# Encoder of a fusion kernel: the 82 steps of a half turn in another order

## What is computed

```python
def layer(h, p):
    q = heads(h @ wq + bq_); k = heads(h @ wk + bk_); v = heads(h @ wv + bv_)
    scores = jnp.einsum('bhqd,bhkd->bhqk', q, k) / jnp.sqrt(jnp.float32(dk))
    attn = jax.nn.softmax(scores, axis=-1)
    o = jnp.einsum('bhqk,bhkd->bhqd', attn, v)
    o = o.transpose(0, 2, 1, 3).reshape(B, S, D)
    h = _ln(h + o @ wo + bo_, g1_, bn1_)
    ff = jax.nn.relu(h @ w1 + b1_) @ w2 + b2_
    h = _ln(h + ff, g2_, bn2_)
    return (h, None)
```

## Time and profile before

| | us |
|---|---|
| median of 3 runs (4498.93 to 4503.75) | 4498.96 |
| the profiled execution | 4506.42 |
| its span, first to last instruction | 4504.5 |
| encoder, 12 turns from 424.45 to 2048.85 | 1624.40 |

### The profile page before, as it was taken

One profiled execution on the slowest core, in us unless ns is written; L12 is line 12 of the kernel. 1 busy time (PEld: TensorE's weight loads), 2 busy tenths in 40 slices (PEclk: granted clock), 3 DMA queues, 4 the chain that ended last, 5 costly groups with the idle time before them and its releaser, 6 DMA issues. The chain is left out here.

```text
span 4504.5 us, 64423 instructions
## 1 busy us (share of the span) xinstructions
PE 3885.5 (86%) x21850; PEld 2498.8 (55%) x21850; DVE 2225.2 (49%) x3415; ACT 2121.8 (47%) x3230; POOL 1103.8 (25%) x1003
## 2 busy tenths in 40 slices
PE   1799999999999999999865999999999994229998
PEld 1355555555555555555544777666676673217776
DVE  2566666666565666565615544444444441203332
ACT  0255455455454455455423766756755761003332
POOL 5123233233232233233220000000100001154443
PEclk6799999999999999999977999999999997559999
DMA  6323333323323333333105111111111113335554
GB/s 135 113 79 104 106 88 103 107 82 98 102 83 111 91 91 104 101 90 105 56 13 153 30 33 26 30 34 26 30 34 26 30 30 135 113 120 124 127 127 97
DMA packets 267379, 370.19 MB, mean 82 GB/s; under 512 B 49456, under 2 KB 168288, under 8 KB 263712
## 3 DMA queue, kind: packets, MB, share of 16 engines
q1 hardware_dynamic: 234640, 287.09, 22.7%
q0 software_dynamic: 22960, 57.40, 5.9%
q10 hardware_dynamic: 9600, 23.26, 1.6%
HBM read 236.56 MB, written 117.10 MB: 79 GB/s over the span
## 5 line engine op out<-in xcount | busy, mean ns | idle before, releaser
L691 DVE TENSOR_REDUCE mx<-ring 128x2 f32<-128x1024 f32 x768 | 919.5, 1222 | 485.1 <-PE ring L478 482.1
L605 ACT ACTIVATE probs<-ring 128x1024 f32<-128x1024 f32 x768 | 767.6, 1024 | 414.4 <-PE ring L491 413.2
L1430 DVE TENSOR_REDUCE a_nmx<-a_ring 128x1 f32<-128x561 f32 (+1 forms) x480 | 341.7, 737 | 308.9 <-PE a_ring L1271 159.4
L1320 ACT ACTIVATE a_ring<-a_ring,a_nmx 128x561 f32<-128x561 f32 (+1 forms) x480 | 333.8, 695 | 197.5 <-DVE a_nmx L1430 195.0
L478 PE MATMUL ring<-k_stack,q_stack 48*128 48x512 f32 x1536 | 359.7, 480 | 55.2 <-DVE mx L691 23.2
L491 PE MATMUL ring<-q_stack,k_stack 64*128 64x512 f32 x1536 | 358.1, 484 | 54.8 <-DVE mx L691 39.5
L505 PE MATMUL acc<-probs,vals 128*32 128x512 f32 x3072 | 396.3, 636 | 1.3 <-ACT probs L605 1.3
L1201 POOL TENSOR_SCALAR_AFFINE_SELECT a_probs<-a_probs 128x256 f32<-128x256 f32 (+1 forms) x240 | 91.9, 383 | 1221.2 <-ACT a_probs L1352 1221.2
L1352 ACT ACTIVATE a_probs<-a_ring 128x561 f32<-128x561 f32 (+1 forms) x480 | 287.3, 637 | 169.5 <-PE a_ring L1268 166.5
L1268 PE MATMUL a_ring<-a_k_hh,a_q_hl 128*128 128x256 f32 (+1 forms) x960 | 311.2, 339 | 22.7 <-DVE a_q_hl L1410 11.0
L491 PEld LDWEIGHTS ring<-q_stack,k_stack 64*128 64x128 f32 x1536 | 140.3, 189 | 282.2 <-DVE mx L691 97.7
(11 more groups left out here) (215 smaller groups left out, 6788.6 us busy)
## 6 DMA issues: line engine op xcount, KB each, us to landing
q_stack<-qk_scratch SPq DMA_DIRECT2D x576, 64.0 KB, 2.4
k_stack<-qk_scratch SPq DMA_DIRECT2D x576, 64.0 KB, 2.4
qk_scratch<-qk_hi SPq DMA_DIRECT2D x32, 768.0 KB, 3.6
qk_scratch<-qk_lo SPq DMA_DIRECT2D x32, 768.0 KB, 5.2
a_q_hm<-a_q_hl SPq DMA_DIRECT2D x48, 280.5 KB
a_k_hh<-a_k_hh SPq DMA_DIRECT2D x48, 280.5 KB
h_in<-tokens SPq DMA_DIRECT2D x34, 384.0 KB, 4.2
res<-tokens SPq DMA_DIRECT2D x32, 384.0 KB, 3.4
```

The lines of the kernel that those rows point to most:

```text
L605: nc.scalar.activation(probs[n % 2][:, pair:pair + 2, x // 2, :], buf[:, :, :], ACT.Exp, scale=DK ** -0.5).then_inc(act, 1)
L691: nc.vector.tensor_reduce(mx[s][:, i, :].rearrange("p (r t) -> p r t", r=2)[:, :, t], buf[:, :, :], AX, ALU.max).then_inc(dve, 1)
L1320: nc.scalar.activation(buf, buf, ACT.Exp, bias=nmx[0:r, i, h:h + 1], accum_out=sums[0:r, i, h:h + 1]).then_inc(act, 1)
L1430: nc.vector.tensor_reduce(nmx[0:r, i, h:h + 1], flat(buf)[0:r, 0:N], AX, ALU.max, negate=True).then_inc(dve, 1)
```

## The change

One string. Each letter stands as often as before, and the steps of each stream keep their order among themselves; no instruction is added or taken away inside the loop.

```diff
-ORDER = "jeehemehememhmepemhemheepheejeppmemememmfepmmfefmjmpjemmfmffefmepemfemfmmpmfmfjjfp"
+ORDER = "ehehejhmemehemhejempememehmpememeemfeppeemfemfmjempemfmfmpfemfmjefmmfmfmmfemppjfpj"
```

## The result

The changed kernel takes 4586.42 us (median of 4 runs, 4581.46 to 4597.36), the kernel before 4500.58 on the same chip (4 runs, 4498.93 to 4503.75). The ratio is 1.0191, 95% interval 1.0173 to 1.0209: 86 us slower, where 58 slower was predicted.

What follows compares the result with a forecast made beforehand. TensorE was taken to set the encoder's pace, with short ring-buffer waits and clock loss. Half turn +12, SyncE's queue +16 and clock +30 made +58 us on the 4498.96 median: 4557 us, range 4495 to 4600.

Steps and rivals of the forecast that it cites:

- rival 1: Longer half turn, weight-load wait and more clock loss all occur: 4557 us, range 4530 to 4590; chance 0.45.
- Part 1: Encoder half turn at full clock: 66.55 us instead of 66.13, +0.4 each, +12 us over 29; bounds 0 and +26.
- Part 2: SyncE's queue: later qk 2 delays bv, first projection of even half turns waits 1.15 us, 14 times: +16 us, bounds 0, +30.
- Part 3: TensorE's clock falls in nearly every half turn after a longer thin stretch ahead of ft: +1.05 us each, +30; bounds 0, +51.
- The walk: Stepping through the new order with step prices and the buffer-ring rule: first projection 11.15, yn 18.45, ft 25.5 us.
- The chain from `yn` to `ft`: From normalization yn, through three GpSimd sweeps, to the start of transposes ft: 7.02 us.
- the sum behind `ft`: Priced steps from ft to the half turn's end: 40.4 us plus 0.65 for a buffer wait, 41.05, against 38.52 before.
- q + 26.3: SyncE's queue: issue of the last stack, counted in us from the start q of the last projection, qk 2.
- The second: Clock falls no more often than before, costing 1.55 us a half turn; order and weight-load costs alone, 4527 us; chance 0.22.
- The third: Faster: VectorE reaches yn by 16.9, ft starts at 24.0, half turn 65.0 us, clock as before: 4483 us; chance 0.13.
- The fourth: No difference: waits only change places and SyncE's loads land in time; within 9 us of 4499; chance 0.12.
- The fifth: Dearer: longer clock fall in each half turn, weights 2.1 us late; 12 + 30 + 51 = +93, 4592 us; chance 0.08.

Runs made afterwards that it cites:

- run 12: Changed kernel with bqk loaded first on its own semaphore (no bv wait) and eight extra matmuls a half turn ahead of ft: 4503.88 us, ratio 0.9998.
- run 10: Kernel before with four extra matmuls a half turn, three ahead of place 35 and one ahead of 37: 4471.28 us, ratio 0.9934.
- run 11: Changed kernel without the bv wait, ln 1 at place 20 instead of 25, six extra matmuls a half turn: 4458.87 us, ratio 0.9899.
- run 1: Changed kernel with bqk loaded first on its own semaphore, TensorE waiting for wv and bv only at step v: 4543.93 us, ratio 1.009.
- run 7: Changed kernel without the bv wait, with twelve extra matmuls a half turn at places 30 to 35: 4518.09 us, ratio 1.0041.
- run 8: Changed kernel without the bv wait, ln 1 at place 20 instead of 25, eleven extra matmuls a half turn: 4490.39 us, ratio 0.9979.
- run 5: Control: kernel before with bqk loaded first on its own semaphore and TensorE waiting for the weights at step v: 4496.4 us, ratio 0.9999.
- run 3: Changed kernel with ln 1 moved from place 25 to 20, nothing else: 4546.9 us, ratio 1.0093.
- run 9: Changed kernel with the last projection, qk 2, moved from place 63 to 54, nothing else: 4602.07 us, ratio 1.0215.

## Why the prediction was right, and where its sizes were off

The direction, the three mechanisms and the range held, though the time lies near its upper end: 4586 of at most 4600, and rival 1, with all three parts, ended at 4590. The sum was 28 us short. Parts 1 and 2 both came out above their own upper bounds, and that the clock came out 8 us below its term, which made up for some of it, was luck. In the changed kernel's 70.69 us a half turn: 67.24 is the order with the clock up (run 12), 2.3 / 2 = 1.15 the wait for `bv`, and the rest, 2.30, the clock. Against the kernel before (66.13, none, 1.55) this is +1.11, +1.15 and +0.75, in 29 half turns 32, 33 and 22 us, together 87. The medians give nearly the same in another way: the order's price is 29 us (run 12 against run 10), the wait 32, and of the 86 this leaves 25 for the clock.

**Part 1, the undisturbed half turn: right in sign, mis-sized.** Predicted +0.4 us and 12 in all, inside bounds of 0 and 26; shown are 1.0 to 1.1 us and 29 to 32 in all, above the upper bound. The walk ran ahead by 0.4 us already at the first projection (11.15 walked, 11.56 in the profile), kept that distance to `yn` (18.45, 18.84) and `ft` (25.5, 25.85), and then lost 0.3 more behind `ft`: 41.05 walked, 67.23 - 25.91 = 41.32 measured in run 12. The chain from `yn` to `ft` was exact, 7.02 and 7.01. So the terms that failed are the head's, "the first projection (place 16) can start at 11.15", and the sum behind `ft`; which prices in them are short is not shown. The step that makes the order dear, `yn` behind three maxima, was the right one: run 11 with `yn` early takes 65.97 a half turn, run 12 without it 67.24. That is 37 us in 29 half turns; the two ratios differ by 0.0109, 49 us, and the rest isn't accounted for.

**Part 2, SyncE's queue: the mechanism right, the wait half as long as it is.** Predicted 1.15 us in 14 turns, 16 us, with an upper bound of 30; shown 2.3 and 32. The term is in the rows. A passage like most others, with `qk` 2 starting at q = 840.57 and the wait 2.25 us:

```profile
866.08 1.36 SPq L848 DMA_DIRECT2D k_stack<-qk_scratch  x3
868.25 0.41 SPq L853 DMA_DIRECT2D tokens<-h_out  x1
...
874.80 0.50 PE L441 MATMUL ring<-hT_hi,wqk_hi 128*128 128x512 f32 x1 [2.25 <-DMA bv_rows<-in_bv]
```

The spill was put at q + 3.0 and is at 2.96. The 16.8 us for three stacks run, in the earlier trace rows, from the first issue to the end of the last, 958.00 + 1.45 - 942.67; so q + 26.3 in the prediction is where the queue should be through with them. It is through at 867.44, q + 26.87: 0.6 later. Then the prediction let the store follow at once, but it is issued only 0.81 us after that, at q + 27.7. From there the 6.5 us "from the store's issue to bv's landing" hold, 874.80 - 868.25. So `bv` lands 1.4 us later than predicted, TensorE is ready for it 0.3 later (q + 31.98 instead of 31.65), and 1.15 become 2.25. The term that failed is the time of the queue between the spill and the store. In the passage of the longest wait (q = 557.12) one issue of the stacks took 2.76 us at 571.50 where the others take 1.26 to 1.56, and the store stands at q + 28.9. In the odd half turns nothing waits for SyncE, as predicted.

**Part 3, the clock: right that it falls in each half turn, too much for it.** Predicted +1.05 us a half turn and 30 in all; the rows leave +0.75 and 22. It falls behind the stretch ahead of `ft` in all 24 half turns, where the kernel before has 16 with a clock below 1.00. But it isn't dearer there: an odd half turn loses 68.74 - 67.24 = 1.5 on average, no more than the kernel before lost on average and 1.1 less than the 2.6 taken. The even ones lose 72.64 - 67.24 - 2.3 = 3.1, and in five of twelve the clock falls twice, first directly behind the wait for `bv`. Part 2 and part 3 therefore aren't independent terms, and run 1, which removed the wait, got 42 us back and not 32. So the fall behind `ft` came more often and no deeper. That the thin work ahead of it brings it about is shown by runs 7, 8, 11 and 12, which fill it and have no fall in 24 half turns; that it came more often *because* the stretch is 1.3 us longer isn't shown, since no run changes its length alone. The size of this term is uncertain by the 13 us that run 5 shows from one profiled execution to another.

Of the page cited in the prediction, the two rules can now be weighed. The stretch from 529.00 holds no idle time of TensorE longer than the 1.55 us ahead of `ft`, and the clock fell behind this stretch in each half turn; filling its gaps in run 12 kept it up. "TensorE: Matmul & The Clock Gate" of the Trainium skill, section "Why this matters for your kernels", which asks for no long unbroken gap, would have given 4527 by the prediction's own count and doesn't agree with these rows. Its section "A second HAM failure mode: psum-queue depth-cycling", on frequent short idles, agrees.

**The rivals.** The second (clock no worse, 4527) falls: the clock falls in 24 of 24 half turns and costs 2.30 us, where it took 1.55 to stay. The third (faster, `yn` early) didn't happen, since `yn` came at 18.84; made to happen in run 3 its half turn was right to 0.35 us, and its time wrong by over 60 us, for it took the clock to stay as it was and the wait to cost 16 us instead of 32. The fourth had parts 1 and 2 at zero; neither is. The fifth (4592) is the nearest in time, in part by luck. Its wait was right: 30 us in 14 turns are 2.1 us each, and 2.3 were measured. But its part 1 was 20 us too low and its clock 29 too high.

What stays open: why the clock falls in some half turns and not in others that are alike in work, in the kernel before behind `ft` (16 of 24) and in the changed one behind the wait for `bv` (5 of 12); and why moving `yn` early alone brings falls ahead of `ft` in odd half turns too. Runs 8 and 11 show only that extra work at the right places removes them.

## What to carry to other kernels

Price a reordering in three separate sums: the walk at full clock, the queues that the moved steps' DMAs stand in (with the gap between the end of one issue and the next, here 0.8 us ahead of the store, and not only the landing), and the clock; then check whether a wait found in one makes another dearer. Where TensorE sets the pace and its clock falls, look at the thin stretches ahead of each fall before moving anything: four matmuls a half turn that compute nothing were worth 0.66%, nine (partly at other places) were worth nothing, so fill only gaps that are idle anyway. And a step moved away from a queue it blocks lands beside something else: run 9 lost more at the new place than it had saved at the old.

## What the runs showed of the hardware that was not expected

A stretch of 5.5 us in which TensorE is busy 3.24, with no idle time over 1.55, was followed by a granted clock of 0.56 over the next 3.6 us, and the same stretch with 5.06 us busy by 1.00.

An idle time of 2.0 to 3.3 us of TensorE, the wait for one load, was followed over the next 6 us by a clock of 0.72 in five half turns of twelve and of 1.00 in seven. Its length doesn't decide: behind 2.17 us the clock was 0.72, behind 2.29 it was 1.00.

Extra matmuls paid for themselves up to a point only. In the kernel before, a half turn took 66.21 us with 4 of them and 67.49 with 9, against 67.68 with none; in the new order without the wait for `bv` it took 67.24 with 8 and 68.00 with 12, both at a clock of 1.00, against 69.12 with none.
